# Layer 0, second half: LayerNorm's scales from GpSimd's power instead of ScalarE's root and VectorE's Newton step

## The reference

```python
def gnn_layer(x, W, b, src, dst):
    h = x @ W.T + b
    msgs = h[src]
    agg = jax.ops.segment_sum(msgs, dst, num_segments=N_NODES)
    return jax.nn.relu(agg)
...
h = jnp.maximum(_layernorm(x, axis=-1), 0.0)
x = x + _L0_gnn_ref(h, edge_index, L0_gnn_W1, L0_gnn_b1, L0_gnn_W2, L0_gnn_b2)   # two gnn_layers
h = jnp.maximum(_layernorm(x, axis=-1), 0.0)                                     # eps 1e-5
x = x + _L1_gnn_ref(h, ...)
```

## Time and profile before

| stage | stretch of the profile, us | PE busy in it |
|---|---|---|
| ordering | 0 to 505 | |
| layer 0, first half (`a_`) | 505 to 835 | 97% |
| layer 0, second half (`b_`) | 835 to 1303 | 79% (to 1310) |
| layer 1, 2, 3 | 1303 to 3079 | 94 to 97% |

### The profile page before, as it was taken

How to read it: one execution, slowest core, us unless ns; L and a number is a source line. 1 busy time by engine, 2 the same in 40 slices (tenths; PEclk the granted TensorE clock), 3 DMA queues, 4 the chain that set the end, 5 groups by cost and what they waited for, 6 DMA issues and landing times. The chain is left out here.

```text
span 3079.1 us, 53053 instructions
## 1 busy us (share of the span) xinstructions
PE 2630.2 (85%) x13954; PEld 2200.3 (71%) x13954; DVE 2067.9 (67%) x5788; ACT 1360.6 (44%) x2818; POOL 1797.1 (58%) x2075
## 2 busy tenths in 40 slices
PE   1257754999788788689999996999999969999998
PEld 1134433788677667578999996888888858888887
DVE  5855546566455555547787876888888856666666
ACT  0045542444354445355555553333333325555554
POOL 4645553555445545467777774787777745555554
PEclk9999999999999889889999998999999989999999
DMA  9944004233333334343333332343334335555554
GB/s 266 320 153 160 5 19 156 86 107 116 117 105 112 118 116 129 115 127 114 110 119 110 118 111 85 117 132 114 114 111 117 106 98 153 152 152 153 153 152 119
DMA packets 147528, 387.65 MB, mean 126 GB/s; under 512 B 35383, under 2 KB 36343, under 8 KB 146842
## 3 DMA queue, kind: packets, MB, share of 16 engines
q0 software_dynamic: 101408, 304.38, 33.3%
q1 hardware_dynamic: 44970, 80.12, 7.8%
q10 hardware_dynamic: 1056, 2.10, 0.2%
HBM read 261.74 MB, written 149.28 MB: 133 GB/s over the span
## 5 line engine op out<-in xcount | busy, mean ns | idle before, releaser
L1524 PE MATMUL c_pu<-c_Zhi,parts 128*128 128x256 f32 x640 | 184.2, 288 | 10.1 <-DVE c_Zlo L1449 10.1
L1526 PE MATMUL c_pu<-c_Zhi,parts 128*128 128x256 f32 x640 | 183.6, 287 | 0.0
L1525 PE MATMUL c_pu<-c_Zlo,parts 128*128 128x256 f32 x640 | 182.4, 285 | 0.0
L800 POOL DMA_INDIRECT f_Gsrc<-rows,indexS x80 | 78.9, 987 | 166.7 <-PE f_phsrc L2020 161.4
L804 POOL DMA_INDIRECT rows<-b_rows,indexD x80 | 80.6, 1008 | 154.2 <-DVE b_rows L899 134.4
L1962 DVE TENSOR_TENSOR f_Hlosrc<-f_phsrc,f_Hhisrc 128x512 fp32r<-128x512 f32 x80 | 55.4, 692 | 167.6 <-ACT f_Hhisrc L1932 124.1
L1938 ACT ACTIVATE f_Mhi<-f_pm 128x512 fp32r<-128x512 f32 x80 | 47.9, 599 | 265.8 <-DVE f_pm L1971 259.1
L804 POOL DMA_INDIRECT h<-a_rows,indexD x80 | 80.7, 1009 | 127.4 <-ACT a_rows L1102 119.6
L1686 ACT CAST d_Hhi<-d_ph 128x512 fp32r<-128x512 f32 x80 | 46.8, 585 | 226.9 <-PE d_ph L1800 222.5
L1242 PE MATMUL b_pt<-b_sel,b_G 128*128 128x128 f32 x640 | 96.1, 284 | 56.5 <-issue 39.1
L1056 ACT CAST b_Thi<-b_pt 128x512 fp32r<-128x512 f32 x80 | 46.9, 586 | 212.8 <-DVE b_pt L773 103.4
(11 more groups left out here) (436 smaller groups left out, 10250.1 us busy)
## 6 DMA issues: line engine op xcount, KB each, us to landing
rows<-n_xt SPq DMA_DIRECT2D x80, 260.0 KB
n_xt<-in_x SPq DMA_DIRECT2D x80, 256.0 KB
h<-q_zerorow SPq DMA_DIRECT2D x80, 256.0 KB
selrowsD<-selD SPq DMA_DIRECT2D x1, 2640.0 KB
selrowsS<-selS SPq DMA_DIRECT2D x1, 2640.0 KB
q_keyrowD<-in_dst POOLq DMA_DIRECT2D x1, 2560.0 KB
q_keyrowS<-in_src POOLq DMA_DIRECT2D x1, 2560.0 KB
o_wstage<-in_L_W ACTq DMA_DIRECT2D x2, 1024.0 KB
```

Source lines behind the costliest of these rows:

```text
L800: return pool.indirect_dma_start(out, None, table, bass.IndirectOffsetOnAxis(ap=rows, axis=0))
L1524: pe.matmul(psum_u[:, o, :], g.Whi[2][:, c, cols], Zhi[:, c, :], start=c == 0, stop=False)
L1525: pe.matmul(psum_u[:, o, :], g.Whi[2][:, c, cols], Zlo[:, c, :], start=False, stop=False)
L1526: ins = pe.matmul(psum_u[:, o, :], g.Wlo[2][:, c, cols], Zhi[:, c, :], start=False, stop=c == C - 1)
```

## The change

The class `RootNorm` goes, and the second half uses `Norm` with the bias on POOL. DVE's six small operations and ACT's root for each pair of tiles become two small operations on DVE (`finish`) and two on POOL (`scales`). POOL's queue is written in another order: for each pair it does the scales of tiles u-2 and u-1, then store, `b_G`, `b_xr`, store, `b_G`, `b_xr`. A tile is stored one step earlier (offset -2 instead of -3), and the `b_G` of tile u+4 now stands behind the scales of the pair that ends with u-1. The constant -0.5 is set in both halves.

```diff
-        ln = RootNorm(e, "ln") if second else None
+        ln = Norm(e, "ln", True) if second else None
...
+            def scales(T):
+                s = T.slot(U)
+                ln.make_scales(pool, T, neg_half, rows[:, s:s + 2, SCALE])
+                ln.make_biases(pool, T, rows[:, s:s + 2, SCALE], rows[:, s:s + 2, BIAS])
...
             def body(i):
-                for u in range(U):
-                    if not second:
+                for pair in (0, 2):
+                    if second:
+                        at(i, pair, -2, U, NT, scales)
+                    for u in (pair, pair + 1):
                         at(i, u, -2, U, NT, store)
-                    at(i, u, 4, U, NT, start_fetch)
-                    if second:
-                        at(i, u, 2, U, NT, residual)
-                        at(i, u, -3, U, NT, store)
+                        at(i, u, 4, U, NT, start_fetch)
+                        if second:
+                            at(i, u, 2, U, NT, residual)
...
-                pool.memset(ln.eps[:, :], LN_EPS).then_inc(s_const, 1)
+            pool.memset(neg_half[:, :], -0.5).then_inc(s_const, 1)
...
-                        if u % 2:
-                            at(i, u, -3, U, NT, roots)
...
-                        at(i, u, -1, U, NT, aggregate_rows)
+                        at(i, u, -1, U, NT, finish_rows)
                         at(i, u, -1, U, NT, pick_node)
-                        if u % 2:
-                            at(i, u, -3, U, NT, scale_rows)
```

More of the change, by code:

```diff
@@ L851, in make_biases @@
         pool.tensor_tensor(biases, self.minus[:, s:s + 2], scales, ALU.mult).then_inc(self.s_bias, 1)
[L854 to L899, removed]
@@ L935, in layer0 @@
             brow = e.sb("brow", [P, D], F32)
+        neg_half = e.sb("neghalf", [P, 2], F32)
         G = e.ring("G", U, [P, D if second else EXT], F32)
@@ L1038, in _ @@
                     pool.memset(rows[:, s, BIAS + 1:EXT], 0.0).then_inc(s_const, 1)
-            pool.wait_ge(s_const, 3 + U if second else 2)
+            pool.wait_ge(s_const, 3 + U if second else 3)
             straight(GR, 1, 1, body, between=W and (lambda n: W.split_low(pool, n)))
@@ L1092, in hot_column @@
                     .then_inc(e_hotq, 1)
-            def roots(T):
-                ln.roots(nc, act, T)
             def relu(T):
@@ L1157, in norm_rows, with finish_rows @@
                 ln.statistics(dve, T, rows[:, T.slot(U), 0:D])
[L1159 to L1164, removed]
+            def finish_rows(T):
+                ln.finish(dve, tick, T)
             def list_nodes(T):
@@ L1196, in body @@
                     if second:
-                        at(i, u, -1, U, NT, aggregate_rows)
+                        at(i, u, -1, U, NT, finish_rows)
                         at(i, u, -1, U, NT, pick_node)
-                        if u % 2:
-                            at(i, u, -3, U, NT, scale_rows)
             dve.wait_ge(s_brow, 16)
-            dve.wait_ge(s_const, 3 + U if second else 2)
+            dve.wait_ge(s_const, 3 + U if second else 3)
             if second:
```

## The result

The changed kernel takes 3002.83 us, median of 4 runs (2999.4 to 3005.29), against 3079.34 us (3074.0 to 3083.37) for the kernel before on the same chip. The ratio is 0.9755, 95% interval 0.9739 to 0.9772: 76.5 us faster. I had forecast 43 us less (3035 us), and the fast end of my range was 3016 us. The direction was right, the size was not, and the measured time lies outside the range, on the fast side.

What follows compares the result with a forecast made beforehand. Late PE signals under POOL's dense DMAs were taken to bound the second half; POOL's 9.7 us plus 0.5 us gives 10.2 against 11.43 us a pair, over 35 pairs 3078 - 43 = 3035 us; range over the cases 3016 to 3104.

Steps and rivals of the forecast that it cites:

- What bounds the stage: Layer 0's second half: PE's signals come late while POOL issues DMAs without a break; 11.43 us a pair against PE's 8.28.
- POOL's floor: POOL's queue: six DMAs in 7.69 us plus 2.0 us added by power and bias make 9.7 us a pair.
- I allow 0.5 us: Lateness left in the second half despite POOL's pauses: 0.5 us a pair above POOL's 9.7, giving 10.2 us.
- l: Lateness of PE's signal to DVE and POOL, 8.8 us in one traced case; expected near 4.3 us after the change.
- my loop 7.55 + l/2: Time a pair by the loop of two pairs from edge sum through store and gather to the next tile, in us.
- The sum: A pair takes the largest of PE, POOL and loop, put at 10.2 us: 1.23 us saved, -43 us over 35 pairs.
- My floor case: Fast end of the likeliest case: POOL's floor alone sets the pair, 35 x 1.73 = 61 us saved, 3017 us.
- DVE's waits for "remote": Sign of being right: waits of DVE's L770 for "remote" below 60 us in the stretch, 116.2 us before.
- Worth nothing by itself: Removing ACT's root (298 ns) and six DVE operations (1.2 us) a pair saves nothing itself, since PE's work hides it.
- Slower, by the tile less in hand: Rival, 0.35: POOL's power waits for the variance, l/2 in each pair; 11.95 us a pair, +21 us, 3099 us.
- A smaller gain: Rival, 0.13: stalls stay in part, a pair takes 10.6 to 11.2 us; 19 us saved, 3059 us.
- No change: Rival, 0.14: PE's gaps do not hang on POOL's DMAs (instruction fetch or byte limit); 11.2 to 11.7 us, 3078 us.

Runs made afterwards that it cites:

- e1: Kernel before plus an idle power and multiply (128x2) on POOL ahead of each pair's first store; 3005.34 us, ratio 0.9763.
- e10: Kernel before plus one idle multiply on POOL ahead of every store, pauses of 2 x 0.8 us a pair; ratio 0.9809.
- e5: Kernel before plus one idle multiply on POOL per pair, a pause of 0.8 us; ratio 0.9996.
- e9: Kernel before plus two idle multiplies on POOL per pair, a pause of 1.05 us; ratio 1.002.
- e13: Kernel before plus one idle power on POOL per pair, a pause of 1.35 us; ratio 0.9961.
- e18: e14 with the six Newton operations done idly on VectorE, on a chip with the kernel before at 3064.78 us; 2990.23 us, ratio 0.9758.
- e14: Kernel before without root and Newton step, VectorE writing variance and negated mean into the rows; POOL's order as before, no operations added there; 2996.80 us, ratio 0.973.
- e2: Changed kernel without its power and multiply on POOL, VectorE writing its two results into the rows, new order kept; 3100.66 us, ratio 1.0071 to the kernel before.
- e15: e14 with the six Newton operations done idly on VectorE, on a chip where the kernel before takes 2899.08 us; ratio 0.9977.
- e17: e14 with the store released as late as before by one more VectorE operation, on the chip with the kernel before at 2899.08 us; ratio 0.9981.
- e7: Kernel before with the gather of x cut to 64 of 512 columns, as many DMAs; ratio 1.002.
- e4: Kernel before without the gather of x in this stage, four DMAs a pair; ratio 0.9627.

## Why the prediction was right in direction and wrong in size

**What bounds the stage.** Right. POOL's dense DMAs make PE's signals late, POOL then stands at the store, and PE falls to 0.90 of its clock. e1 and e10 show it: thin out the DMAs by an idle operation and the stage gains, with all else left alone. By what way dense DMAs delay a signal stays unknown.

**POOL's floor, "+2.0 us, 9.7 us a pair".** This term was mis-sized, by 0.4 us a pair. The terms measured: 0.02 us before the power (I had 0.50 from a row of layer 1, where POOL waited), 0.74 for it (0.70), 0.08, 0.20, 0.86 (0.83), less 0.30: 1.6 us, and 7.69 + 1.6 = 9.3 us a pair. The rows show 9.31.

**"I allow 0.5 us" for lateness.** This step failed, and is the larger part of the miss. I took it that stalls above the floor would remain in proportion, between full stalls and none. The runs show a step: 9.3 us in nearly every pair with the pause, 11.2 to 11.6 on average with a pause that is too short (e5, e9, e13) or with none. What remained above the floor was nothing, not 0.5 us. l is 3.0 and 2.9 us in the rows after the change, under the 3.5 us at which my loop 7.55 + l/2 would reach 9.3. So 10.2 us, for which I took l = 5.3, is the time of neither state.

**The sum.** (11.43 - 9.31) x 35 = 74 us instead of 43; measured in S: 73.9. That the two agree so closely is partly luck: 7.9 of the 73.9 us fall behind the last `b_G`, where I had counted nothing. My floor case, "61 us saved", would have been 74 us and 3004 us with the right gap, beside the 3002.83 measured; with the gap as I had it, the range ended short of it. One sign that I had named did not hold: DVE's waits for "remote" were to fall below 60 us in the stretch, and are 96.9 us in 350. In e1 they are fewer, 62.7 us in 300, and it is no faster for that.

**"Worth nothing by itself".** For VectorE's six operations e18 bears it out. For the whole of what is taken off VectorE and ScalarE, with the earlier release of the store that comes with it, e14 refutes it: 0.973 without GpSimd's help. I had priced the engines' busy time and found the chain to the store hardly changed, 4.8 us against 4.95, and had not asked what another release does to a loop that is stable in one state and not in the other.

**The rivals.** "Slower, by the tile less in hand" is real in e2: 3100.66 - 3081.68 = +19 us, where I had worked out +21; the pause covers it. That the numbers are near each other is luck: mine took 8.8 us of lateness in every pair, and e2 has 15 such waits in 300 us, of up to 11.3 us. I gave it 0.35 because I weighed order and pause apart; they act together. "A smaller gain" took it that stalls stay in part; in the changed kernel none of the long ones is left. "No change", by PE's fetch of instructions, falls: PE's gaps go when GpSimd's DMAs thin out, with PE's program untouched (e1). The Trainium skill, "GPSIMD Engine Reference", section "4.1 Engine selection", gives elementwise work to VectorE. The rows agree in kind, 0.74 us for a power on POOL against about 0.16 us for a Newton operation on DVE, but that did not decide: in this stage the time that POOL spent was what the kernel needed.

**On which chip.** The gain belongs to chips with late signals. On the chip of e15 to e17 a pair takes 8.3 us with nothing on GpSimd between the DMAs; the change's POOL floor of 9.31 us would make it slower there by about 40 x 1.0 = 40 us. This is an estimate; the changed kernel did not run there.

**Open.** What makes the signals late, and why on some chips only; whether the number of DMAs or of their rows counts; why the step lies between 1.35 and 1.6 us, and whether a bound near 9.2 us a pair stands behind it; which part of e14 acts.

## What to carry to other kernels

Where a queue runs into stalls that feed themselves, compare the states of the loop, not its mean: add an idle operation of known length at the suspected queue before rewriting anything, and if pure delay makes the kernel faster, the way in which that queue issues is what costs. Look at each turn of the loop, since 11.4 us on average were turns of 7.7 and of 15. Take the gap ahead of an added instruction from a row where its engine did not wait. A gain from pacing should be timed on several chips, since it can be one chip's cure and another's load.

## What the runs showed of the hardware

- A pause of 1.6 us of GpSimd in every 9.3 us took 76 us off the kernel (e1); 1.35 us took 8 (e13).
- Where GpSimd can issue six indirect DMAs in 7.7 us, VectorE waits up to 8.2 us for a signal of PE (11.3 us in e2), whether the stretch carries 77 GB/s (e7) or 114 (the kernel before); with four a pair none of its waits ends with "remote" (e4).
- One chip showed none of this in three kernels, at 163 GB/s and six DMAs in 8.3 us (e15 to e17).
- On GpSimd a 128x2 power takes 0.74 us and starts within 0.02 us behind an indirect DMA; the next DMA starts 0.86 us behind a compute operation, and 0.30 us behind a DMA.
